# Four samples per feature product, with the products spread between table lookups, in a recommendation tower on one core

## The chip, the cores and the metric

The kernel runs on one core of one Trainium2 chip. The metric is device time in microseconds, the median of several executions. The core has TensorE (PE, matmuls), VectorE (DVE), ScalarE (ACT), GpSimd (POOL) and SyncE (SP, which only starts DMAs); each has its own in-order queue, and they meet through semaphores. Matmuls write PSUM; all other tiles are in SBUF.

## The reference

2048 samples. Each has a dense vector of 128 numbers and 26 table indices; the 26 rows looked up and the dense vector make 27 features. All 351 dot products of two different features, with the dense vector, are the 479 inputs of a three-layer perceptron.

```python
e = jnp.stack([tbl_0[ids[:, 0]], ..., tbl_25[ids[:, 25]]], axis=1)     # 2048 x 26 x 128
all_emb = jnp.concatenate([bottom_output[:, None, :], e], axis=1)      # 2048 x 27 x 128
gram = jnp.einsum('bfd,bgd->bfg', all_emb, all_emb)
z = gram[:, _TRIU_I, _TRIU_J]                                          # 351 pairs
h = jnp.concatenate([z, r_bottom_output], axis=1)
h = jnp.maximum(h @ W_top1 + b_top1, 0.0)                              # 479 -> 512
h = jnp.maximum(h @ W_top2 + b_top2, 0.0)                              # 512 -> 256
y = h @ W_top3                                                         # 256 -> 1
```

Twelve tables have 1000 rows, the others 1250 to 125000. Everything is float32.

## The kernel before

The batch is four blocks of 512 samples, each four tiles of 128. `features` holds all 27 features of a block with the 128 dimensions on the partitions: `[128, tile, sample, feature]`.

**Two ways to look up.** 18 tables are gathered: one indirect DMA on GpSimd (line 368) fetches 128 rows into `rows` (a ring of two tiles), TensorE transposes them in groups of four (`transpose_group`, line 403), and ScalarE copies each group into `features` (line 577). The other 8 tables of 1000 rows are looked up by a product (`onehot_lookups`, lines 421 and 422): the table is loaded whole (`table_raw`, 125 partitions of 4 KB, line 264) and split in a high part (ScalarE, line 596) and a low part (VectorE, line 716); the wanted indices of 512 samples are loaded on all partitions (`wanted`, line 272) and compared with the row numbers into eight one-hot chunks (seven on VectorE, line 732; one on ScalarE, lines 605 and 611); 8 chunks x 2 parts are 16 matmuls of 512 columns, and ScalarE copies the result straight into `features` (line 627). The first block looks up 12 tables in this way, four of them for 384 samples only. `table_raw` is a ring of two; a load waits until the low part of the table two before is taken.

**Products.** `gram_tile` makes one small product per sample, 26 x 26 (line 442), four samples side by side in the four 32-row quadrants of PSUM. TensorE runs all 128 of a tile in a row, and the four tiles of a block one behind the other:

```python
for i in range(P):
    at = QUADRANT * (i % 4)
    last = pe.matmul(gram[at:at + GRAM, q % 2, i // 4, 0:GRAM],
                     features[:, q, i, 0:GRAM], features[:, q, i, 1:SLOTS], start=True, stop=True)
```

ScalarE (two or three of the quadrants) and VectorE then copy columns of the products to the partitions where layer 1 wants them (`regroup`, lines 557 and 559: five copies per quadrant, one of 10 x 320 and four of 128 columns), and three small DMAs of SyncE (line 293) move the columns that don't fit. VectorE splits the result in high and low (`split_tile`), for four input tiles `pairs` plus the dense vector.

**Layers.** Layer 1 is 4 outputs x 5 inputs x 3 matmuls of 512 columns (lines 449 to 451), layer 2 is 2 x 4 x 3, the output layer two float32 products (line 509).

**Order.** It is written out by hand per block, in a hardware loop over blocks: four product tiles; then the 8 lookups of the next block; then the layers of this block; the transposes are tucked in between. PSUM holds two groups of transposes, two tiles of products and two accumulators `acc`.

## Time and profile before

| | |
|---|---|
| median of 3 runs | 464.12 us (463.21 to 467.48) |
| profiled execution, first to last instruction | 643.8 us (its own time: not given apart from this span) |
| mean granted TensorE clock in it | 0.759 |
| instructions in it | 13317 |

The profile is of one other execution, in which every instruction leaves a record. Its span is 180 us longer than the timed runs, so its stages must be weighed one by one before they are compared with 464.12 us; the section on the prediction does that.

### The profile page before, as it was taken

Reading aid. Unit: us, or ns where it says so; the run is one execution under the profiler, and the core shown is the slowest. Engines: PE = TensorE matmul, PEld = TensorE weight load, DVE = VectorE, ACT = ScalarE, POOL = GpSimd, SP = SyncE. Lnnn points to the kernel's source line nnn. Section 1 sums busy time; section 2 is a strip of 40 time slices with the busy share of each in tenths; the row PEclk is TensorE's granted clock in tenths of the full one; section 3 lists DMA queues with packets and bytes.
Section 4 is the critical chain, followed back from the end, with each engine's and each line's share of the span. In section 5 each row is a group of like instructions: output and inputs, shape, how many; then the busy total and the mean of one; then the engine's idle time right before and its main releaser. Section 6 shows DMA issues by size and latency. Waiting matters only on the chain.

```text
span 643.8 us, 13317 instructions
## 1 busy us (share of the span) xinstructions
PE 395.4 (61%) x5324; PEld 296.7 (46%) x5324; DVE 235.1 (37%) x472; ACT 310.4 (48%) x470; POOL 285.1 (44%) x282
## 2 busy tenths in 40 slices
PE   2686572353578947625367894733536799467487
PEld 2464461232466835214256673412325578335375
DVE  3574560033286411030347822002135782202451
ACT  2484660056489512223559751412456983028832
POOL 7777357556003754664600573555550067250000
PEclk9798785565699987756568998955556899677689
DMA  5558442111224411111123441111121331010000
GB/s 157 165 184 230 168 139 58 38 40 44 91 98 134 144 41 43 45 47 36 49 81 109 152 126 29 51 42 43 41 68 57 132 114 50 25 42 6 8 4 0
DMA packets 21925, 50.39 MB, mean 78 GB/s; under 512 B 7288, under 2 KB 7320, under 8 KB 21744
## 3 DMA queue, kind: packets, MB, share of 16 engines
q1 hardware_dynamic: 12902, 30.96, 14.5%
q0 software_dynamic: 8832, 18.11, 10.6%
q8 instruction: 45, 0.74, 0.5%
q10 hardware_dynamic: 138, 0.52, 0.2%
q14 instruction: 8, 0.07, 0.0%
HBM read 49.00 MB, written 0.01 MB: 76 GB/s over the span
## 4 chain that ended last, share of the span: by engine, by line
PE 37%; issue 25%; another core or an unknown queue 13%; DMA 11%; ACT 9%; DVE 3%; SPq 0%; ACTq 0%; DVEq 0%
DMA table_raw<-in_tbl 11%; PE gram L442 11%; PE acc L421 5%; PE turned L403 5%; PE acc L422 4%; PE acc L449 4%; PE acc L451 4%; PE acc L450 3%; ACT pairs L559 3%; ACT table_hi L596 2%; DVE table_lo L716 2%; ACT features L577 1%; PE acc L509 1%; DVE onehot L732 1%
## 5 line engine op out<-in xcount | busy, mean ns | idle before, releaser
L368 POOL DMA_INDIRECT rows<-in_tbl,index x276 | 284.4, 1030 | 292.3 <-PE turned L403 157.0
L442 PE MATMUL gram<-features 128*26 128x26 f32 x4096 | 94.9, 213 | 151.8 <-issue 150.1
L421 PE MATMUL acc<-onehot,table_hi 125*128 125x512 f32 (+1 forms) x288 | 127.1, 441 | 50.2 <-DVE table_lo L716 22.7
L442 PEld LDWEIGHTS gram<-features 128*26 128x26 f32 x4096 | 70.7, 128 | 185.6 <-issue 183.3
L577 ACT COPY features<-turned 128x512 f32<-128x512 f32 (+2 forms) x80 | 82.2, 1062 | 139.4 <-remote 102.7
L422 PE MATMUL acc<-onehot,table_lo 125*128 125x512 f32 (+1 forms) x288 | 121.6, 422 | 0.0
L732 DVE TENSOR_SCALAR onehot<-wanted,row_number 125x512 fp32r<-125x512 int32 (+1 forms) x252 | 104.2, 475 | 33.7 <-PE acc L422 20.1
L557 DVE COPY aside<-gram 10x320 f32<-10x320 f32 x21 | 15.5, 737 | 234.6 <-remote 177.2
L421 PEld LDWEIGHTS acc<-onehot,table_hi 125*128 125x128 f32 x288 | 60.9, 211 | 71.8 <-issue 38.4
L559 ACT COPY pairs<-gram 18x128 f32<-18x128 f32 (+3 forms) x172 | 67.2, 390 | 1.5
L422 PEld LDWEIGHTS acc<-onehot,table_lo 125*128 125x128 f32 x288 | 60.9, 211 | 10.8
L403 PE MATMUL turned<-identity,rows 128*128 128x128 f32 x276 | 56.4, 322 | 12.8 <-issue 7.6
L557 ACT COPY aside<-gram 10x320 f32<-10x320 f32 x43 | 31.3, 729 | 63.7 <-remote 42.6
L716 DVE TENSOR_TENSOR table_lo<-table_raw,table_hi 125x1024 fp32r<-125x1024 f32 x36 | 44.0, 1223 | 49.2 <-ACT table_hi L596 37.2
L596 ACT CAST table_hi<-table_raw 125x1024 fp32r<-125x1024 f32 x36 | 38.3, 1064 | 35.3 <-DMA table_raw<-in_tbl 34.9
L403 PEld LDWEIGHTS turned<-identity,rows 128*128 128x128 f32 x276 | 37.3, 162 | 21.3 <-issue 12.5
L627 ACT COPY features<-acc 128x512 f32<-128x512 f32 (+1 forms) x36 | 42.2, 1172 | 6.2 <-PE acc L422 5.3
L649 ACT ACTIVATE h<-acc,b_sb 128x512 f32<-128x512 f32 x16 | 10.7, 687 | 59.0 <-remote 37.5
L771 DVE CAST onehot<-h 128x512 fp32r<-128x512 f32 x16 | 7.0, 437 | 75.8 <-ACT h L649 50.9
L449 PE MATMUL acc<-onehot,w_hi 128*128 128x512 f32 x32 | 16.5, 516 | 26.6 <-ACT h L649 26.6
L559 DVE COPY pairs<-gram 18x128 f32<-18x128 f32 (+1 forms) x84 | 32.4, 385 | 0.9
L611 ACT ACTIVATE onehot<-distance,row_number 125x512 fp32r<-125x512 f32 (+1 forms) x36 | 25.6, 712 | 14.3 <-PE acc L422 11.8
(40 smaller groups left out, 302.1 us busy)
## 6 DMA issues: line engine op xcount, KB each, us to landing
table_raw<-in_tbl SPq DMA_DIRECT2D x35, 500.0 KB
wanted<-in_onehot_ids SPq DMA_DIRECT2D x36, 256.0 KB
rows<-in_tbl,index POOLq DMA_INDIRECT x276
aside<-in_w SPq DMA_DIRECT2D x1, 1280.0 KB
bottom<-in_xT SPq DMA_DIRECT2D x4, 256.0 KB
h<-in_w SPq DMA_DIRECT2D x1, 512.0 KB
table_raw<-in_tbl ACTq DMA_DIRECT2D x1, 500.0 KB
pairs<-aside SPq DMA_DIRECT2D x16, 20.0 KB
```

Source lines behind the costliest of these rows:

```text
L368: pool.indirect_dma_start(out=rows[:, q % RING, f, :], out_offset=None, in_=gathered[f], in_offset=bass.IndirectOffsetOnAxis(ap=index[q // ...
L403: last = pe.transpose(turned[:, n % 2, i, :], rows[:, q % RING, first + i, :], identity[:])
L421: pe.matmul(to, table_hi[0:ROW_PARTS, i % TABLE_RING, c, :], of, start=(c == 0), stop=False)
L422: last = pe.matmul(to, table_lo[0:ROW_PARTS, i % TABLE_RING, c, :], of, start=False, stop=(c == CHUNKS - 1))
L442: last = pe.matmul(gram[at:at + GRAM, q % 2, i // 4, 0:GRAM], features[:, q, i, 0:GRAM], features[:, q, i, 1:SLOTS], start=True, stop=True)
L449: pe.matmul(to, w_hi, x_hi, start=first, stop=False)
L557: copy(to(aside, 0, ASIDE, ASIDE), of(ASIDE, 1, ASIDE))
L559: last = copy(to(pairs, QUADRANT * j, COLUMN_ROWS[j], PAIR_TILES), of(COLUMN_ROWS[j], COLUMNS_FROM[j], PAIR_TILES))
L577: nc.scalar.copy(features[:, q % BLOCK_TILES, :, 1 + first:1 + first + size].rearrange("d b f -> d f b"), turned[:, n % 2, 0:size, :]).the ...
L596: nc.scalar.copy(table_hi[0:ROW_PARTS, i % TABLE_RING], table_raw[0:ROW_PARTS, i % 2]).then_inc(table_high, 1)
L716: dve.tensor_tensor(table_lo[0:ROW_PARTS, i % TABLE_RING], table_raw[0:ROW_PARTS, i % 2], table_hi[0:ROW_PARTS, i % TABLE_RING], ALU.subtr ...
L732: dve.tensor_scalar(onehot[0:ROW_PARTS, c, samples], wanted[0:ROW_PARTS, i % 2, samples], row_number[0:ROW_PARTS, c:c + 1], None, ALU.is_e ...
```

## The change

1. **Four samples per product.** `features` becomes `[128, ring of 4 tiles, pair of samples, feature, 2]`. `gram_chunk` multiplies the 4 x 27 features of four samples with their 4 x 26 features: one product of 108 x 104 in place of four of 26 x 26; only its four diagonal blocks are used. A tile is 32 products in 4 chunks of 8.
2. **Products leave through DRAM.** Each chunk is copied whole (107 partitions x 832) to `products`, two chunks of a tile by VectorE and two by ScalarE; four DMAs per tile store the diagonal blocks into a DRAM tensor `square`, and nine DMAs per part load them back as layer 1 wants them (three input tiles instead of four).
3. **Eleven lookups by product in every block** (44 in place of 36), so 15 gathered tables per tile (240 gathers in place of 276). A lookup's result is copied to a block buffer `looked`, and from there, when a block's lookups are done, one ScalarE copy per tile (`place`, 11 x 128) puts it into `features`.
4. **A table comes in two DMAs**, of 112 and 13 partitions. Its ring is three deep, and the low part is written over the raw table, so a load waits for the end of the lookup three before. The weights no longer share tiles with other data.
5. **An order for all engines.** `order()` lists the steps of the whole kernel, unrolled: the first block's 11 lookups; then the 16 chunks of a block, with a lookup of the next block, a slice of the layers of the block before (one output of layer 1, layer 2) or the output layer ahead of each chunk; a group of transposes goes in where a table of lengths says its rows have landed. The last block's chunks have only layers ahead of them, and its layers run in two halves of 256 samples; the load of the second half's pairs waits for the output of the first half, since the second layer's result lies in the same tile.

```diff
-ONEHOT = [3, 4, 9, 13, 14, 17, 20, 21]
-RING = 2
-PAIR_TILES = 4
+ONEHOT = [3, 4, 9, 13, 14, 17, 20, 21, 22, 23, 24]
+LOOKUPS = (11, 11, 11, 11)
+HIGH_RING = 2
+LOW_RING = 3
+WANTED_RING = 3
+PACK = 4
+CHUNK_GROUPS = 2 * BANK_GROUPS
+PAIR_TILES = 3
...
+LENGTH = {"lookup": 38, "gram": 16, "layer1": 27, "layer2": 52, "output": 15, "turn": 5, "place": 0}
...
+        if b == 0:
+            before = spread(lookups(1, 0, LOOKUPS[1]), len(chunks))
+        elif b < BLOCKS - 1:
+            before = (lookups(b + 1, 0, FIRST_LOOKUPS) + layers(b - 1)
+                      + behind(("output", b - 1, 0), lookups(b + 1, FIRST_LOOKUPS, LOOKUPS[b + 1])))
+        else:
+            before = [[]] * (TILE_CHUNKS + 1) + layers(b - 1) + [[("output", b - 1, 0)]]
...
-        features = sb("features", [P, BLOCK_TILES, P, SLOTS])
+        features = sb("features", [P, FEATURE_RING, P // 2, SLOTS, 2])
+        looked = sb("looked", [P, MOST, BLOCK])
...
+            of = onehot_tables[i].rearrange("(p c) d -> p c d", c=CHUNKS)
+            for at in (slice(0, EVEN_PARTS), slice(EVEN_PARTS, ROW_PARTS)):
+                eng.dma_start(table_raw[at, n % LOW_RING], of[at]).then_inc(raw_landed[n % LOW_RING], 16)
+        def store_place(eng, t, s):
+            eng.dma_start(square[b % 2, q, s],
+                          products[SLOTS * s:SLOTS * s + GRAM, t % PRODUCTS_RING, s].rearrange("f g t -> f (g t)")
...
+        def load_triple(eng, part, i):
+            eng.dma_start(pairs[row:row + n, first:end].rearrange("f q s k t -> f (q s) (k t)"),
+                          square[b % 2, first:end, :, 0:n, (g - 1) * RUN:(g - 1 + PAIR_TILES) * RUN].rearrange(
+                              "q s f n -> f (q s) n")).then_inc(pairs_landed, 16)
...
+                for i in range(CHUNK_GROUPS):
+                    at = (i % BANK_GROUPS) * WIDE
+                    a, e = divmod(j * CHUNK_GROUPS + i, 2)
+                    of = features[:, t % FEATURE_RING, a * PACK:(a + 1) * PACK, :, e]
+                    last = pe.matmul(gram[0:PACK * SLOTS, n % 2, i // BANK_GROUPS, at:at + WIDE],
+                                     of.rearrange("d s f -> d (s f)"), of[:, :, 1:SLOTS], start=True, stop=True)
...
+        def take_products(copy, t, j):
+            return copy(
+                products[0:LAST_ROW, t % PRODUCTS_RING, :, :, first:first + CHUNK_GROUPS].rearrange(
+                    "f s g (k t) -> f (s g) k t", k=2),
+                gram[0:LAST_ROW, n % 2, :, 0:BANK_GROUPS * WIDE].rearrange("f k (t n) -> f n k t", n=WIDE))
...
+            def place(t):
+                nc.scalar.copy(features[:, t % FEATURE_RING, :, SLOTS - LOOKUPS[b]:SLOTS, :].rearrange("d u f e -> d f u e"),
+                               looked[:, first:MOST, q * P:(q + 1) * P].rearrange("d f (u e) -> d f u e", e=2)
+                               ).then_inc(placed, 1)
```

What stands in a row on the engines, at three places. First TensorE. Before, the end of the loop's products in the first tile of a block, with the jump to the next pass (`ISA` and `REGISTER_ALU` rows only set up waits):

```order
L400 REGISTER_ALU
L403 MATMUL turned<-identity,rows 128x128 x4
L442 MATMUL gram<-features 26x26 x16
L398 ISA
L400 REGISTER_ALU
L403 MATMUL turned<-identity,rows 128x128 x2
L442 MATMUL gram<-features 26x26 x48
L543 REGISTER_ALU
L543 COMPARE_AND_BRANCH
```

Now, between two lookups of block 2 and with products of block 1:

```order
L457 MATMUL acc<-onehot,table_hi 128x512
L458 MATMUL acc<-onehot,table_lo 128x512
L469 MATMUL turned<-identity,rows 128x128 x4
L484 MATMUL gram<-features 108x104 x8
L469 MATMUL turned<-identity,rows 128x128 x4
L457 MATMUL acc<-onehot,table_hi 128x512
```

The products stood in long runs with nothing but transposes between them; now a chunk of eight stands behind every lookup or slice of a layer.

Second SyncE. Before, the moves of a tile's columns, inside the loop:

```order
L293 DMA pairs<-aside 10x512
L293 DMA pairs<-aside 6x512
L293 DMA pairs<-aside 2x256
L246 REGISTER_ALU
L264 DMA table_raw<-in_tbl 125x1024
```

Now, where the pairs of block 0 are loaded:

```order
L330 DMA table_raw<-in_tbl 112x1024
L330 DMA table_raw<-in_tbl 13x1024
L342 DMA pairs<-square 26x16x96
L342 DMA pairs<-square 24x16x96
L342 DMA pairs<-square 20x16x96
L342 DMA pairs<-square 18x16x96
L342 DMA pairs<-square 14x16x96
L342 DMA pairs<-square 11x16x96
L342 DMA pairs<-square 8x16x96
L342 DMA pairs<-square 5x16x96
L342 DMA pairs<-square 2x16x96
L361 DMA wanted<-in_onehot_ids 128x512
```

Nine loads stand in one piece in the queue that also brings the tables and the wanted indices.

Third ScalarE. Now, at the change from block 0's lookups to its products:

```order
L575 CAST table_hi<-table_raw 125x1024
L562 COPY features<-turned 128x4x64x2
L603 COPY features<-looked 128x11x64x2 x4
L581 ACTIVATE distance<-wanted,row_number 125x512
L586 ACTIVATE onehot<-distance,row_number 125x512
```

The four copies of `place` stand in a row, ahead of the one-hot chunk of a later lookup. Before, such copies were spread, one behind each lookup (line 627).

## Rows read from the trace of the kernel before

**Rows 1.** The page: busy us of each engine (share of span), instructions.

```profile
PE 395.4 (61%) x5324; PEld 296.7 (46%) x5324; DVE 235.1 (37%) x472; ACT 310.4 (48%) x470; POOL 285.1 (44%) x282
```

**Rows 2.** Windows by stage: length, busy time (instructions) per engine, clock, DMA share, GB/s.

```profile
0.00:90.00 90.00, 55.27 (x224) 44.12 (x227) 50.90 (x101) 51.69 (x61) 58.82 (x57) 0.89 0.56 172
90.00:175.00 85.00, 34.21 (x1057) 24.29 (x1058) 17.95 (x35) 30.75 (x56) 46.01 (x46) 0.57 0.23 66
175.00:249.50 74.50, 59.71 (x248) 46.64 (x248) 37.59 (x75) 41.19 (x56) 27.77 (x27) 0.89 0.29 91
249.50:332.30 82.80, 36.94 (x1065) 24.55 (x1064) 16.09 (x33) 33.52 (x60) 44.06 (x46) 0.58 0.20 58
...
566.50:611.00 44.50, 26.25 (x1065) 18.37 (x1064) 10.87 (x24) 28.71 (x54) 8.95 (x10) 0.73 0.08 19
611.00:643.80 32.80, 26.28 (x119) 20.51 (x112) 10.92 (x22) 8.86 (x17) 0.00 (x0) 0.89 0.01 3
```

**Rows 3.** Timeline, TensorE, product stages: start, length, engine, line, [idle before].

```profile
406.91 0.41 PE L442 MATMUL gram<-features 128*26 128x26 f32 x32
...
417.36 0.29 PE L442 MATMUL gram<-features 128*26 128x26 f32 x3 [1.18 <-issue]
...
602.86 1.74 PE L442 MATMUL gram<-features 128*26 128x26 f32 x127 [2.47 <-issue]
```

**Rows 4.** Chain that ended last, from 0 to 90 us: shares, then start, length.

```profile
by line: DMA table_raw<-in_tbl 60.4%; issue 11.7%; DVE table_lo L716 6.9%; ACT table_hi L596 5.9%; PE acc L421 4.2%; PE acc L422 3.9%; DVE onehot L732 2.7%; ACT features L627 1.0%; SPq L272 0.8%; SPq L299 0.5%; SPq L297 0.5%; PE turned L403
...
2.15 11.75 DMA table_raw<-in_tbl
...
57.45 14.80 DMA table_raw<-in_tbl
```

**Rows 5.** Chain from 185 to 200 us: start, length.

```profile
193.86 6.64 DMA table_raw<-in_tbl
```

**Rows 6.** Lines by form: busy us, mean ns of one, idle before and its releasers.

```profile
L368 POOL DMA_INDIRECT rows<-in_tbl,index x276 | 284.4, 1030 | 292.3 <-PE turned L403 157.0 <-issue 79.0 <-DMA index<-in_ids 41.4
...
L577 ACT COPY features<-turned 128x512 f32<-128x512 f32 x61 | 71.8, 1197 | 106.7 <-remote 72.4 <-PE turned L403 33.0 <-ACT y_sb L665 1.2
...
L716 DVE TENSOR_TENSOR table_lo<-table_raw,table_hi 125x1024 fp32r<-125x1024 f32 x36 | 44.0, 1223 | 49.2 <-ACT table_hi L596 37.2 <-issue 11.9
...
L596 ACT CAST table_hi<-table_raw 125x1024 fp32r<-125x1024 f32 x36 | 38.3, 1064 | 35.3 <-DMA table_raw<-in_tbl 34.9 <-issue 0.2
...
L403 PEld LDWEIGHTS turned<-identity,rows 128*128 128x128 f32 x276 | 37.3, 162 | 21.3 <-issue 12.5 <-ACT features L577 2.5
...
L557 ACT COPY aside<-gram 10x320 f32<-10x320 f32 x43 | 31.3, 729 | 63.7 <-remote 42.6 <-PE gram L442 20.8
...
L559 ACT COPY pairs<-gram 18x128 f32<-18x128 f32 x43 | 18.4, 428 | 0.0
...
L649 ACT ACTIVATE h<-acc,b_sb 128x512 f32<-128x512 f32 x16 | 10.7, 687 | 59.0 <-remote 37.5 <-PE acc L451 21.5
```

**Rows 7.** Timeline, VectorE: the seven one-hot chunks of a lookup.

```profile
338.98 2.86 DVE L732 TENSOR_SCALAR onehot<-wanted,row_number 125x512 fp32r<-125x512 int32 x7
```

**Rows 8.** Timeline, TensorE at 352 us: lookup matmuls around four transposes.

```profile
352.58 0.39 PE L422 MATMUL acc<-onehot,table_lo 125*128 125x512 f32 x1
352.81 0.60 PE L403 MATMUL turned<-identity,rows 128*128 128x128 f32 x4
353.16 0.47 PE L421 MATMUL acc<-onehot,table_hi 125*128 125x512 f32 x1
353.48 0.40 PE L422 MATMUL acc<-onehot,table_lo 125*128 125x512 f32 x1
```

**Rows 9.** Timeline, TensorE: the float32 product of the output layer.

```profile
408.77 1.45 PE L509 MATMUL acc<-aside,w_sb 128*1 128x512 f32 x3
```

**Rows 10.** Timeline at the end: SyncE's moves of columns, VectorE behind them.

```profile
615.52 2.14 SPq L293 DMA_DIRECT2D pairs<-aside  x3
...
618.82 0.43 DVE L762 CAST pairs_hi<-pairs 128x512 fp32r<-128x512 f32 x1 [2.19 <-DMA pairs<-aside]
```

More of the change, by code:

```diff
@@ L88, with groups_of, products_and_others, lookups @@
 ACT = mybir.ActivationFunctionType
-def dlrm_tower(nc, xT, ids, onehot_ids, row_numbers, gathered, onehot_tables, w1, b1, w2, b2, w3, out):
+def groups_of(t):
+    n = TABLES - LOOKUPS[t // BLOCK_TILES]
+    return [min(GROUP, n - g) for g in range(0, n, GROUP)]
+LENGTH = {"lookup": 38, "gram": 16, "layer1": 27, "layer2": 52, "output": 15, "turn": 5, "place": 0}
+FIRST_LOOKUPS = 5
+GATHER_LENGTH = 14
+GATHER_START = 60
+def products_and_others():
+    def lookups(b, first, last):
+        return [[("lookup", b, i)] for i in range(first, last)]
+    def layers(part):
+        return [[("layer1", part, m)] for m in range(M1)] + [[("layer2", part, 0)]]
+    def behind(output, others):
+        return [[output] + others[0]] + others[1:]
+    def spread(others, n):
+        places = [[] for _ in range(n)]
+        for i, other in enumerate(others):
+            places[i * n // len(others)] = other
+        return places
+    steps = [step for place in lookups(0, 0, LOOKUPS[0]) for step in place]
+    for b in range(BLOCKS):
+        first = b * BLOCK_TILES
+        steps += [("place", first + q, 0) for q in range(BLOCK_TILES)]
+        chunks = [("gram", first + q, j) for q in range(BLOCK_TILES) for j in range(TILE_CHUNKS)]
+        if b == 0:
[5 more added lines that the diff above has]
+            before = [[]] * (TILE_CHUNKS + 1) + layers(b - 1) + [[("output", b - 1, 0)]]
+        for i, chunk in enumerate(chunks):
+            steps += before[i] if i < len(before) else []
+            steps.append(chunk)
+    for part in range(BLOCKS - 1, len(PARTS)):
+        steps += [step for place in layers(part) for step in place] + [("output", part, 0)]
+    return steps
@@ new lines, with accumulations @@
+ORDER = order()
+LOOKUP_STEPS = [step for step in ORDER if step[0] == "lookup"]
+def accumulations():
+    number = {}
+    for kind, b, i in ORDER:
+        if kind in ("lookup", "layer1", "output"):
+            number[kind, b, i] = len(number)
+        if kind == "layer2":
+            for m in range(M2):
+                number[kind, b, m] = len(number)
+    return number
+FILL = accumulations()
+PAIRS_AFTER = {("gram", (b + 1) * BLOCK_TILES, 1): b for b in range(BLOCKS - 1)}
+PAIRS_AFTER["gram", TILES - 1, 0] = len(PARTS) - 2
@@ new lines, in load_pairs @@
+            def load_pairs(part):
+                b, first, end = PARTS[part]
+                for t in range(b * BLOCK_TILES + end - PRODUCTS_RING, b * BLOCK_TILES + end):
+                    sp.wait_ge(square_landed[t % PRODUCTS_RING], (t // PRODUCTS_RING + 1) * PACK * 16)
+                if part:
+                    sp.wait_ge(acc_out, FILL["output", part - 1, 0] + 1)
+                for i in range(len(TRIPLES)):
+                    load_triple(sp, part, i)
+            load_index(0)
+            load_wanted(0)
@@ new lines, in output @@
+            def output(part):
+                fill, (b, first, end) = FILL["output", part, 0], PARTS[part]
+                act.wait_ge(accumulated, fill + 1)
+                at_least(act, out_landed, 16 * part)
+                nc.scalar.copy(y_sb[:, 0:width(part)].rearrange("o (q a s e) -> o q s a e", q=end - first, s=PACK, e=2),
+                               acc[0:1, fill % 2, 0:width(part)].rearrange("o (q s a e) -> o q s a e", q=end - first, s=PACK, e=2)
+                               ).then_inc(acc_out, 1)
+                act.wait_ge(acc_out, fill + 1)
+                at = b * BLOCK + first * P
+                act.dma_start(out[:, at:at + width(part)], y_sb[:, 0:width(part)]).then_inc(out_landed, 16)
```

959 lines of the change are left out of this document (410 added, 549 removed).

## The prediction

> **What bounds the kernel now.** I read the windows by stage first, then the chain of waits, then the lines by form. Over the whole span no engine is full: TensorE 61%, ScalarE 48%, GpSimd 44% [rows 1]. The windows [rows 2] show why: stages with different limits. In the first 90 us TensorE is busy for 55. Each later block is a product stage of 83 to 85 us with TensorE busy for 34 to 37 at a granted clock of 0.57 (mostly the lower level, 1.2 GHz), and then lookups and layers, 74.5 us with 59.7 busy at 0.89. The last product stage takes 44.5, the tail 32.8.
>
> The span is 643.8 us and the median 464.12, so 180 us of the profile are not in the timed runs. All other stages together are 90 + 3 x 74.6 + 32.8 = 347 us (the third window of lookups repeats the first), the product stages 297. In these, 32 product records run in 0.41 us, 10.6 ns apart up to the next group, and elsewhere three records end a wait of 1.18 us for nothing that the profile shows [rows 3]. This is the only stage with enough such waiting to lose 180 us, so I put the loss there: the timed runs have 464 - 347 = 117 us for four product stages and for whatever lies outside the span, 27 to 29 us a block. ScalarE's work in such a stage is 31 to 33.5 us, and 28.7 in the last [rows 2]: it sums to 126, as much as is left for them. So in the timed runs the copies behind the products fill the product stage, while TensorE needs 1024 records x 10.6 ns = 11 us of it per block. What lies outside the span is then small; I take 8 us, between 0 and 15.
>
> The first 90 us hang on the tables: 60.4% of the chain there is the load of tables, one of them 14.80 us, where a table alone later takes 6.64 [rows 4, 5].
>
> **The change part by part**, made against the 347 + 117 us above.
>
> *Step lengths at the upper clock.* Lookup matmuls start 0.233 us apart [rows 8] (352.58 to 352.81), so a lookup is 16 x 0.233 = 3.73 us. Four transposes put 353.48 - 352.81 - 0.233 = 0.44 us between them, 0.11 each, 1.65 for a tile of 15. A layer matmul has the same 512 columns: layer 1 is 48 x 0.233 = 11.2, layer 2 24 x 0.233 = 5.6. Float32 records of 512 columns take (1.45 - 0.16) / 3 = 0.43 us, with 0.16 for the pipeline's end [rows 9], so the output layer's four are 1.7.
>
> *The product.* The trace has no 108 x 104 product. At 0.84 ns per column [rows 9] a record of 104 columns is 87 ns, two per product. Whether the 108-column weight load hides is the question: around a float32 transpose of 128 columns it does, nearly (107 ns at that rate, 110 measured [rows 8]). I take 90 ns: a chunk is 16 x 0.09 = 1.44 us, a block 23.0, the kernel 1024 x 0.09 = 92 us. Bounds: 87 ns, and 162 ns more, the mean of a transpose's weight load [rows 6], if it is never hidden. I take the transposes' spacing, the nearest row. Before, the quadrants overlapped and TensorE needed 44 us; so its own work grows by 48 us here.
>
> The Trainium skill speaks against this part. "TensorEngine Tiling (Array Packing)", sections Available Configurations and Performance Considerations: an array cut into four column tiles of 32 works on them independently, up to four times as fast for a small output dimension. By that rule the change gives the factor of four up. The 10.6 ns of [rows 3] for what would be 22 ns in a row at 0.84 ns a column agree in direction. The same page says that copying PSUM out may then become the bound, and the 126 us of ScalarE agree with that too.
>
> *Copies out of the products.* Before, a tile was four copies of 320 (0.729 us) and sixteen of 128 (0.428) [rows 6]: up to 9.8 us. The two sizes give 1.57 ns per element and 0.23 fixed; 832 elements are 1.54 us, and 1.8 at the feature copy's rate (1.197 us for 512); I take 1.65, four per tile 6.6, shared by two engines. Bounds: 1.0 us, by the unstrided ReLU of 512 in 0.687 [rows 6], and 1.9 us. ScalarE's share falls from some 100 us to 32 x 1.65 = 53. They now have 5 to 6 us of other TensorE work between them, so at either bound they are hidden.
>
> *Eight more lookups, 36 fewer gathers.* A lookup costs TensorE 3.73 us. Gathers cost GpSimd (284.4 + 79.0) / 276 = 1.32 us [rows 6]; 240 are 316 us, continuous, always ahead of the 400 us and more that TensorE takes. Its 157.0 us of waiting for transposes says that it has room.
>
> *First stage.* Three tables are in flight and a ring place is free at a lookup's end: period = (load + high 1.06 + low 1.22 + lookup 3.73) / 3. With loads of 8 us (between 6.64 and 14.80 [rows 4, 5]) it is 4.67 us. VectorE needs 1.22 + 2.86 = 4.1 [rows 6, 7]. So 11 x 4.67 = 51; the first table lands at 2.15 + 6.64 = 9 (the second one before at 13.9 [rows 4]), its parts take 2.3: the stage ends at 63 us, against 90. Bounds: 4.1 and 6 us a lookup, 57 to 78.
> The Trainium skill, "DMA: Bandwidth & Descriptors", section "Why a DMA increments its semaphore by 16 and not by 1": a DMA uses the largest number of engines up to 16 that divides its outermost dimension. 125 partitions would get 5 engines, 112 get 16. By that rule the load is no longer late and the stage goes by VectorE, ending 6 us earlier; the DMA share of 0.56 [rows 2] with late tables doesn't contradict it.
>
> *Blocks.* Block 0's products: 41.0 (lookups) + 23.0 + 6.6 (transposes) = 70.6. Blocks 1 and 2 add 11.2 + 5.6 + 1.7: 89.1 each. The last: 23.0 + 6.6 + 18.5 = 48.1. On top come waits in the sequence: (a) the split of the pairs ahead of layer 1 takes 3 x 1.1 us on VectorE (0.43 [rows 10] and half of a 1.22 us low part [rows 6]) behind a product copy, and TensorE has 0.7 us of bottom work meanwhile: 3 us in each of blocks 1 and 2; (b) four copies of `place` stand in a row on ScalarE; 1408 elements are 1.55 us each unstrided, 2.8 at the 1.197 us per 512 of the feature copy [rows 6]. Behind them waits the one-hot chunk of the lookup after next. From the last lookup's end ScalarE has 0.9 + 1.65 + 6.2 (or 11.2) + 1.4 = 10.2 (15.2) us to it; TensorE's chunk, lookup, chunk and transposes, and 5 of 8 parts of the next lookup, are 9.5: 1 to 6 us. In the last block no lookup covers the first copy: 4 us; (c) handovers. Before, lookups and layers of 8 x 3.73 + 60 x 0.233 + 5.6 + 4 of transposes = 53.5 took 74.5, 21 of waiting; the chunks now fill the ones behind ReLU and split, so I take 3 to 5. Together: 77, 96, 96, 52. VectorE in such a block has 11 x 4.1 + 8 x 1.65 + 9 of splits = 67 us; ScalarE 11 x 3.2 (high 1.06, and abs, one-hot and copy like the ReLU, 0.7 each) + 11 of feature copies + 6 of `place` + 13 of products + 4 of ReLU = 69 us: both below 89.
>
> *SyncE.* Each move of columns costs 2.14 / 3 = 0.71 us of issue [rows 10]; nine loads are 6.4 us, and tables and wanted indices queue behind them. These run three lookups ahead, 17 us, so I cost it at nothing; without that cover it would be 6 us in blocks 1 and 2. Stores wait for their chunks and only delay loads that are early.
>
> *Tail.* Before 32.8. Now two halves in series: 72 matmuls of 256 columns at 0.12 are 8.6, handovers 4, output 0.9: 13.5 each. Between them the loads of the second half's pairs wait for the first half's output: 6.4 + 2.19 + split 1 = 9.6. Sum 37.
>
> Total: 63 + 77 + 96 + 96 + 52 + 37 = 421, and 8 outside: 429, **forecast 430 us**, a gain of 34: 27 from the first stage, and 8 from the rest, 224 + 109 + 33 = 366 before and 77 + 96 + 96 + 52 + 37 = 358 now.
>
> **Rivals.**
> 1. *No waits.* (a) to (c) vanish and tables come by VectorE's pace: 57 + 71 + 90 + 90 + 49 + 34 + 8 = 399 to 412. For it: chunks between all steps. Against: 21 us in 74.5 before. Chance 0.22.
> 2. *ScalarE becomes the bound.* If the pair-wise feature copies stay at 1.8 ns per element, ScalarE has 35 + 17 + 11 + 14 + 4 = 81 us in a block, block 0 goes by it (82), and each block change costs 6: 445 to 457. The block buffer then doesn't do what it should. For it: 1.197 us per 512 in [rows 6], a stride as well. Chance 0.16.
> 3. *Slower than before: weight loads show in the products.* Each product record waits for its load. 34 us over 1024 records are 33 ns: at 123 ns per record it is as slow as before, with half of the 162 ns exposed (171 ns) 430 + 83 = 513. For it: no run of 108-column loads behind such short products is in this trace. Against: the transposes. Chance 0.14, with other losses of that size in the row of steps.
> 4. *The profile's loss is elsewhere.* Then the product stages really take more than 29 us and the gain is larger; this ends in rival 1's range.
>
> **How the numbers follow.** Forecast 430 (418 to 443): 0.48. Rival 1: 0.22, of it 0.05 below 396. Rival 2: 0.16. Rival 3: 0.14, of it a part below 466. The range that leaves out 2 in 10 is 396 to 466. About 1% is what a measurement of this kernel can tell; that is 459.5 and 468.8. Faster by over 1%: 0.48 + 0.22 + 0.16 = 0.86, of which 0.07 goes to no change, since rival 2 ends at that limit; with 0.01 of rival 3 that is 0.79, 0.08 and 0.13 for slower.
>
> **What would show it.** The chunk of eight products 1.4 to 1.5 us long in the timeline; the first chunk at 63 us; copies to `products` about 1.65 us, `place` 1.55; TensorE busy over 85% of the time between 63 us and the last chunk, at a clock near 1; no wait of TensorE for rows; profile and timed runs closer together, since the records fall by more than half. It is wrong if chunks take over 1.9 us, if TensorE waits for ScalarE at each block change by more than 6 us, or if the tail exceeds 45.

## The result and the profile after

The changed kernel takes 438.27 us (median of 4 runs, 431.13 to 439.86), the kernel before 464.59 (4 runs, 463.21 to 467.48): ratio 0.935, 95% interval 0.926 to 0.944. (Executions fall in a faster and a slower state; ratios, here and below, are of the runs in the faster one, medians are of all runs.) Forecast: 430. The profiled execution is the fastest of the four: 431.13 us, of which the span is 429.1.

The page of after: busy time, TensorE in 40 slices, its granted clock, the chain that ended last.

```profile
PE 384.5 (90%) x2348; PEld 325.2 (76%) x2348; DVE 256.1 (60%) x480; ACT 234.2 (55%) x326; POOL 287.6 (67%) x246
...
PE   0999999997699986899999999899999789997847
...
PEclk9999999999699999999999999999999998999979
...
PE 49%; POOL 28%; issue 7%; DMA 6%; DVE 3%; ACT 3%; SPq 3%; DVEq 0%; ACTq 0%; POOLq 0%
```

TensorE went from 61% to 90% [rows 1] and its clock from 0.759 to 0.98. New in the chain is GpSimd with 28%: the gathers.

Windows of after, cut where the first product of each block starts and the last ends (length, busy time of PE, PEld, DVE, ACT, POOL, clock, DMA share, GB/s), beside [rows 2]:

```profile
0.00:63.00 63.00, 51.76 (x222) 41.09 (x223) 52.04 (x105) 42.78 (x58) 48.43 (x42) 1.00 0.83 216
63.00:146.70 83.70, 75.50 (x488) 66.01 (x487) 59.24 (x108) 55.81 (x75) 68.77 (x50) 0.96 0.67 180
146.70:247.70 101.00, 94.23 (x577) 78.99 (x576) 62.65 (x116) 57.02 (x82) 79.06 (x73) 1.00 0.62 155
247.70:341.80 94.10, 90.10 (x559) 75.71 (x557) 55.15 (x101) 53.18 (x78) 74.28 (x66) 1.00 0.55 137
341.80:393.50 51.70, 49.55 (x360) 43.16 (x361) 17.36 (x24) 18.35 (x24) 17.10 (x19) 0.97 0.30 70
393.50:429.10 35.60, 23.34 (x152) 20.22 (x151) 9.71 (x28) 7.12 (x15) 0.00 (x0) 0.90 0.10 25
```

The same stretches were forecast at 63, 77, 96, 96, 52 and 37 us.

Lines by form of after (busy us, mean ns of one, idle before and its releasers), beside [rows 6]:

```profile
L440 POOL DMA_INDIRECT rows<-in_tbl,index x240 | 287.0, 1196 | 76.0 <-issue 71.9 <-DMA index<-in_ids 3.1 <-PE turned L469 0.9
...
L550 DVE COPY products<-gram 107x832 f32<-107x832 f32 x32 | 32.8, 1024 | 51.3 <-PE gram L484 51.2
L562 ACT COPY features<-turned 128x512 f32<-128x512 f32 x48 | 30.9, 644 | 6.3 <-PE turned L469 6.2
L550 ACT COPY products<-gram 107x832 f32<-107x832 f32 x32 | 27.4, 855 | 19.7 <-PE gram L484 19.6
...
L603 ACT COPY features<-looked 128x1408 f32<-128x1408 f32 x16 | 23.2, 1545 | 0.0
```

The gathers, now 240 in place of 276, wait for TensorE for 0.9 us in place of 157.0: GpSimd runs without a stop from 4.6 us to its last gather at 363.4, one gather per 1.50 us. What TensorE waited for in after (us in total, times, longest):

```profile
PE acc L489 <- DVE pairs_lo L717: 13.1, 10, 5.4
PE turned L469 <- DMA rows<-in_tbl,index: 12.6, 5, 6.5
PE acc L457 <- DVE table_lo L675: 10.4, 1, 10.4
PE gram L484 <- issue: 2.4, 1, 2.4
```

Timeline at the end of after: 48 products in a row, the two output layers, and between them SyncE's second load of pairs.

```profile
383.61 9.86 PE L484 MATMUL gram<-features 128*108 128x104 f32 x96
...
406.80 1.02 PE L528 MATMUL acc<-pairs,w_sb 128*1 128x256 f32 x4 [0.57 <-ACT pairs L617]
...
413.82 0.58 PE L489 MATMUL acc<-pairs_hi,w_hi 128*128 128x256 f32 x1 [5.45 <-DVE pairs_lo L717]
...
426.11 1.02 PE L528 MATMUL acc<-pairs,w_sb 128*1 128x256 f32 x4 [0.57 <-ACT pairs L617]
...
408.35 3.33 SPq L342 DMA_DIRECT2D pairs<-square  x9
```

### The profile page after: what moved, and what is told of

Same layout as the page of the kernel before. It is cut to its first block, busy times and chain, and to the rows that moved or that the text cites. A ratio compares the mean times of both kernels' runs of the same rounds, so it can differ in the third digit from the quotient of the medians.

```text
span 429.1 us, 6585 instructions
## 1 busy us (share of the span) xinstructions
PE 384.5 (90%) x2348; PEld 325.2 (76%) x2348; DVE 256.1 (60%) x480; ACT 234.2 (55%) x326; POOL 287.6 (67%) x246
## 4 chain that ended last, share of the span: by engine, by line
PE 49%; POOL 28%; issue 7%; DMA 6%; DVE 3%; ACT 3%; SPq 3%; DVEq 0%; ACTq 0%; POOLq 0%
POOL rows L440 28%; PE gram L484 13%; PE acc L457 8%; PE acc L458 8%; PE acc L489 5%; PE acc L490 5%; PE acc L491 5%; PE turned L469 4%; SPq L342 2%; DMA rows<-in_tbl,index 2%; DMA pairs<-square 2%; DVE pairs_lo L717 2%; PE acc L528 2%; ACT features L603 1%; DVE pairs_hi L715 1%
## 5 line engine op out<-in xcount | busy, mean ns | idle before, releaser
L457 PE MATMUL acc<-onehot,table_hi 125*128 125x512 f32 x352 | 145.0, 412 | 12.3 <-DVE table_lo L675 10.4
L688 DVE TENSOR_SCALAR onehot<-wanted,row_number 125x512 fp32r<-125x512 int32 x308 | 131.2, 488 | 30.2 <-PE acc L458 14.8
L458 PE MATMUL acc<-onehot,table_lo 125*128 125x512 f32 x352 | 140.9, 400 | 0.0
L484 PE MATMUL gram<-features 128*108 128x104 f32 x1024 | 112.4, 263 | 2.4 <-issue 2.4
L484 PEld LDWEIGHTS gram<-features 128*108 128x108 f32 x1024 | 109.2, 180 | 4.5 <-issue 3.4
L550 DVE COPY products<-gram 107x832 f32<-107x832 f32 x32 | 32.8, 1024 | 51.3 <-PE gram L484 51.2
L586 ACT ACTIVATE onehot<-distance,row_number 125x512 fp32r<-125x512 f32 x44 | 31.9, 725 | 45.4 <-PE acc L458 44.7
L469 PE MATMUL turned<-identity,rows 128*128 128x128 f32 x240 | 37.7, 277 | 12.6 <-DMA rows<-in_tbl,index 12.6
L562 ACT COPY features<-turned 128x512 f32<-128x512 f32 x64 | 39.3, 614 | 15.2 <-PE turned L469 15.1
L550 ACT COPY products<-gram 107x832 f32<-107x832 f32 x32 | 27.4, 855 | 19.7 <-PE gram L484 19.6
L581 ACT ACTIVATE distance<-wanted,row_number 125x512 f32<-125x512 int32 x44 | 32.0, 727 | 0.8 <-ACT y_sb L625 0.8
L594 ACT COPY looked<-acc 128x512 f32<-128x512 f32 x44 | 25.6, 583 | 11.1 <-PE acc L458 7.2
```

What stands on the lines that cost most here:

```text
L457: pe.matmul(to, table_hi[0:ROW_PARTS, n % HIGH_RING, c, :], of, start=(c == 0), stop=False)
L458: last = pe.matmul(to, table_lo[0:ROW_PARTS, n % LOW_RING, c, :], of, start=False, stop=(c == CHUNKS - 1))
L469: last = pe.transpose(turned[:, n % 2, i, :], rows[:, t % ROWS_RING, GROUP * g + i, :], identity[:])
L484: last = pe.matmul(gram[0:PACK * SLOTS, n % 2, i // BANK_GROUPS, at:at + WIDE], of.rearrange("d s f -> d (s f)"), of[:, :, 1:SLOTS], start ...
L550: return copy(products[0:LAST_ROW, t % PRODUCTS_RING, :, :, first:first + CHUNK_GROUPS].rearrange("f s g (k t) -> f (s g) k t", k=2), gram ...
L562: nc.scalar.copy(features[:, t % FEATURE_RING, :, 1 + GROUP * g:1 + GROUP * g + size, :].rearrange("d u f e -> d f u e"), turned[:, n % 2, ...
```

## Experiments

All twelve ran where the kernel before took 648.4 to 652.4 us (four groups of 7 to 11 runs, on three chips) and the changed kernel 479.76, not 464.59 and 438.27. What is different there, the runs don't tell. So each time below is read beside those, by its ratio to the kernel before in the same group.

### The changed kernel there (c_after)

> The changed kernel itself, beside the kernel before on the same chip as the three that follow. The runs of the first four experiments had the kernel before at 650 us in place of 464, with TensorE waiting up to 29 us for nothing that the profile shows, so they need a comparison on their own chip. If this chip is like the one of the result: 438 us, ratio 0.935. If it is like that of the first four experiments: before 650, this 470 to 480, ratio 0.73.

479.76 us (472.66 to 484.13); before 648.4; ratio 0.732 (0.726 to 0.737). Most of the 41 us more than in the result lies in one kind of stretch (the longest at 103 to 127 us, another at 180 to 193). Timeline of this run, TensorE, GpSimd and ScalarE:

```profile
104.68 0.40 PE L458 MATMUL acc<-onehot,table_lo 125*128 125x512 f32 x1
...
111.75 0.33 PE L484 MATMUL gram<-features 128*108 128x104 f32 x1 [0.90 <-issue]
111.90 0.94 POOL L440 DMA_INDIRECT rows<-in_tbl,index  x1 [0.30 <-issue]
113.16 0.48 PE L484 MATMUL gram<-features 128*108 128x104 f32 x1 [1.08 <-issue]
...
127.14 1.05 PE L484 MATMUL gram<-features 128*108 128x104 f32 x5 [0.37 <-issue]
127.44 0.72 ACT L586 ACTIVATE onehot<-distance,row_number 125x512 fp32r<-125x512 f32 x1 [20.99 <-remote]
...
127.76 1.77 POOL L440 DMA_INDIRECT rows<-in_tbl,index  x1 [4.93 <-remote]
```

From 103 to 127 us TensorE starts few records, from 106 us on one at a time, at distances that are multiples of 0.70 us, and waits for nothing that the profile shows. The gathers beside it run at their shortest, 0.94 us with 0.30 between. GpSimd stops at 122.8, and TensorE is free again from 127.

TensorE is not the only one that is held. ScalarE's one-hot chunk of 127.44 needed only its own `distance` (through at 106.4) and the end of TensorE's lookup, whose last matmul started at 104.68; it still started 21 us late. VectorE stands for 29.54 us up to 126.46, and GpSimd's wait of 4.93 us can only be for transposes, which were through by 110.0. The gathers' rhythm alone isn't enough either. The window just before has the same rhythm, with TensorE busy for 4.84 of 5 us:

```profile
98.00:103.00 5.00, 4.84 (x33) 3.96 (x31) 0.00 (x0) 0.50 (x1) 3.78 (x4) 1.00 0.77 212
```

The wait named "issue" is 29.4 us of the products here and 2.4 in the result's profile. The name also covers waits with a plain cause: the 2.37 us in the result's profile (at 341.75) end as ScalarE is through with the first copy of `place` (four of them from 340.22), and so do 4.08 us (at 173.65) and 2.37 us (at 388.08) of the 29.4. The trace of the kernel before had stretches of the same kind, and I had not looked at both engines together:

```profile
111.93 0.94 POOL L368 DMA_INDIRECT rows<-in_tbl,index  x1 [0.30 <-issue]
117.70 0.94 POOL L368 DMA_INDIRECT rows<-in_tbl,index  x1 [4.83 <-PE turned L403]
...
113.88 0.20 PE L442 MATMUL gram<-features 128*26 128x26 f32 x1 [1.20 <-issue]
...
116.82 1.22 PE L442 MATMUL gram<-features 128*26 128x26 f32 x82
```

82 records run in 1.22 us in the pause of GpSimd from 112.9 to 117.7, about 3 us into it; while it gathers, from 96 to 113 us, they come in ones to fives.

### Without gathers, both kernels (e11, e12)

```diff
-            for t in range(TILES):          # e11, GpSimd
+            for t in range(ROWS_RING):
-                pe.wait_ge(rows_landed[t % ROWS_RING][g], rows_count(t, g))
+                pe.wait_ge(rows_landed[t % ROWS_RING][g], rows_count(t % ROWS_RING, g))
...
-            with pool.Fori(1, BLOCKS) as b:   # e12: only tiles 0 and 1 of block 0 are gathered
```

> The changed kernel with the gathers of the first two tiles alone (30 of 240); the later tiles use the same rows again, so the 210 other gathers are left out, and all else of the computation stays. On a chip where the kernel before takes 648 us and the changed one 480. Theory (GpSimd has two effects: its gathers set the pace, and while they run back to back TensorE gets one instruction per 0.70 us): both go, TensorE's waits for nothing fall from 29 us to below 5 and those for rows to 0, the time is 405 to 425 us. Rival A (GpSimd sets the pace, but the waits for nothing have another cause): 435 to 460, with 20 us and more of these waits left. Rival B (neither): 470 to 480.

> The kernel before with the gathers of the first two tiles alone (36 of 276); the later tiles use the same rows again, so 240 gathers are left out. Theory (the 150 us of waits for nothing in the products arise only beside back-to-back gathers): they go, and the time falls from 648 us to 430 to 470, what the timed runs of the result had; the product stages are then 27 to 33 us, filled by ScalarE's copies, as the prediction had them for the timed runs. Rival (4096 short products starve TensorE's instruction supply by their number, whatever GpSimd does): 600 us or more. In between: part of the waits has another cause.

e11: 416.45 us (413.23 to 425.56), ratio 0.636 (0.630 to 0.642). e12: 451.69 us (448.14 to 463.56), ratio 0.689 (0.683 to 0.696). Both times are in the range of their theory. The gathers cost the kernel before 200 us and the changed one 63 in this place. TensorE's waits in e11:

```profile
PE acc L489 <- DVE pairs_lo L717: 11.2, 5, 5.5
PE gram L484 <- issue: 2.4, 1, 2.4
```

No wait for rows, and of the waits named "issue" 0.4 us and the 2.4 that belong to `place`, as in the result's profile. In e12 the windows of the four product stages are:

```profile
87.00:119.30 32.30, 19.53 (x1056) 16.07 (x1056) 18.81 (x35) 28.19 (x52) 0.00 (x0) 0.74 0.19 58
184.90:218.00 33.10, 19.73 (x997) 15.36 (x996) 15.88 (x33) 29.87 (x55) 0.00 (x0) 0.75 0.10 32
284.00:319.00 35.00, 20.73 (x1030) 16.30 (x1030) 15.85 (x33) 31.09 (x57) 0.00 (x0) 0.73 0.12 35
382.30:415.80 33.50, 20.53 (x1066) 15.74 (x1065) 10.85 (x24) 28.63 (x54) 0.00 (x0) 0.80 0.03 6
```

32 to 35 us where [rows 2] had 83 and, for the last, 44.5, with ScalarE busy for 28 to 31: undisturbed, the copies fill the product stage. TensorE's waits named "issue" in the products fell from 150.1 to 46.9 us, not to nothing as the theory had it; ScalarE is busy during most of what is left. With the gathers of two tiles alone the change is worth 451.7 - 416.5 = 35 us.

### Fewer and more gathers (e4, e5)

```diff
-ONEHOT = [3, 4, 9, 13, 14, 17, 20, 21, 22, 23, 24]
-LOOKUPS = (11, 11, 11, 11)
+ONEHOT = [3, 4, 9, 13, 14, 17, 20, 21, 22, 23, 24, 25]    # e5: without 24
+LOOKUPS = (12, 12, 12, 12)                                # e5: 10 each
```

> The changed kernel with 12 lookups by product in each block in place of 11, so 14 gathered tables per tile, 224 gathers in place of 240; each block's twelfth lookup stands ahead of the last chunk with the step that was there. Theory (GpSimd's gathers, one per 1.5 us and continuous to 363 us, set the pace now, and TensorE's waits for rows are 12.6 us): 16 gathers fewer free 24 us on GpSimd, while TensorE has 4 lookups more (15 us) and 16 transposes fewer (1.8); the waits for rows go, and the time stays within 1% or falls by up to 5 us. Rival (TensorE is the bound, as predicted, GpSimd has room): slower by 13 us, 0.7 of them in the first stage per 1% of the lookup, so 451 us where the changed kernel takes 438, 3% more.

> The changed kernel with 10 lookups by product in each block, 16 gathered tables per tile, 256 gathers. Theory (GpSimd sets the pace): 16 gathers more are 24 us on GpSimd, the last rows land 24 us later, while the first stage ends 4.7 us earlier: 450 to 460 us where the changed kernel takes 438. Rival (TensorE is the bound): 15 - 1.8 = 13 us faster, 425 us. If both bind by turns: within 1%.

Twelve: 482.41 us, ratio 0.739 (0.735 to 0.744), against 0.732: 13 us more of TensorE work cost 2.7 us by the medians, 1% by the ratios. Ten: 505.33, ratio 0.781 (0.776 to 0.786): 25.6 us slower with 16 gathers more and 13 us of TensorE work less, 1.6 us per gather. Both times are near what the theory said and far from its rival, and eleven is near the balance there. That GpSimd's gathers set the pace by themselves the traces don't show: TensorE's waits for rows are 5.7 us in c_after, 5.1 with twelve and 10.9 with ten, while with ten GpSimd stands 44.4 us for transposes (4.4 in c_after) and TensorE 22 us for ScalarE's copies into `features` (11.6 of them once, for a `place`).

### The two DMAs of a table (e1, e2)

```diff
-            for at in (slice(0, EVEN_PARTS), slice(EVEN_PARTS, ROW_PARTS)):
-                eng.dma_start(table_raw[at, n % LOW_RING], of[at]).then_inc(raw_landed[n % LOW_RING], 16)
+            at = slice(0, ROW_PARTS)
+            eng.dma_start(table_raw[at, n % LOW_RING], of[at]).then_inc(raw_landed[n % LOW_RING], 16)
```

e2 makes the reverse edit in the kernel before.

> The changed kernel with each table in one DMA of 125 partitions in place of two of 112 and 13; nothing else differs. Theory (the two DMAs made the first stage short): a table again takes 11.75 to 14.80 us to land, as in the profile of before; with three tables in flight a lookup of the first stage then takes (11.75 to 14.8 + 1.06 + 1.22 + 3.73) / 3 = 5.9 to 6.9 us in place of 4.7, so the first chunk of products starts at 77 to 88 us in place of 63, and the time is 452 to 463 us. Rival (the third place of the ring and the low part written in place did it, the split of the DMA nothing): within 1% of the changed kernel, 434 to 442 us, the first chunk at 63 us.

> The kernel before, with each table in two DMAs of 112 and 13 partitions, as the change has it; its ring of two tables stays. If the load was what the first 90 us waited for and the split mends it, the first stage goes by VectorE's 4.1 us a lookup and ends near 63 us in place of 90: about 437 us, as fast as the changed kernel, and then all the rest of the change together is worth nothing. If a ring of two keeps the stage at half of the gain: about 450. If the split does nothing: 464.

e1 by its trace: the first products start late, as the theory had it (77 to 88):

```profile
L484 PE MATMUL gram<-features x1024: 256/262/506, 87.5 to 440.9; 128*108 128x104 f32 x171
```

With two DMAs it is 62.4 (e9) and 63 (after), so without the split nearly all of the first stage's gain is gone; ScalarE's waits for tables rise from 16.0 us (after) to 78.6 over the kernel. Yet the time is 477.42 us, ratio 0.734 (0.729 to 0.738), no change. The 25 us are won back in block 0. Its products start at 87.5 us and those of block 1 at 165.0, in c_after at 61.8 and 173.65: e1 has no stretch like the one at 103 to 127, and from 95 to 160 us TensorE is busy for 63.0 of 65 us at a clock of 1.00. So this run shows what the split does to the stage, and not what it is worth in a run like the result's. e2: 640.68 us, ratio 0.985 (0.979 to 0.991), its first products at 84.1 us in place of 90.0. That is less than half of the gain that I had given a ring of two: with two tables in the ring, and TensorE waiting 6.29 us once for nothing that the profile shows and 3.12 for a one-hot chunk, only 6 us of the stage went. The split alone is not enough.

### The order and the packing undone (e3, e10)

```diff
-        for i, chunk in enumerate(chunks):
-            steps += before[i] if i < len(before) else []
-            steps.append(chunk)
+        steps += chunks
+        for place in before:
+            steps += place
```

```diff
+                    for s in range(PACK):
+                        to = gram[QUADRANT * s:QUADRANT * s + GRAM, n % 2, i // BANK_GROUPS, at + s * GRAM:at + (s + 1) * GRAM]
+                        last = pe.matmul(to, of[:, s, 0:GRAM], of[:, s, 1:SLOTS], start=True, stop=True)
```

> The changed kernel with the 16 chunks of a block in one row, ahead of its lookups and layers, so that only the spreading of the products is undone (the dense vectors of blocks 2 and 3 are loaded behind layer 2, where their tile is free). Theory (the spreading is worth what the chunks cover): before, lookups and layers of one block had 21 us of waiting in 74.5 us for ReLU, split and table parts; I expect 5 to 8 us of it back in each of three blocks, so 453 to 462 us. Rival (with copies of 0.86 and 1.02 us per chunk of 1.60 us nothing has to be spread): 434 to 442 us, TensorE without a wait for copies within the row.

> The changed kernel with the products of one sample at a time again, 26 x 26 in the four 32-row quadrants, 4096 records in place of 1024; all the rest (chunks between steps, copies, DRAM, order) stays, and only the packing is undone. (The first two chunks also write the whole of their PSUM banks once, 16 records.) Theory A, as the prediction had it from the 10.6 ns between records: the quadrants overlap, TensorE needs 44 us in place of 102, and the time falls by as much as GpSimd's pace allows, to 400 to 425 us where the changed kernel takes 438. Theory B (many short instructions are what cost the kernel before its product stages of 83 us; TensorE is not supplied with them): slower, 480 us or more, with TensorE's waits for nothing that the profile shows inside the products.

e3: 556.73 us (547.3 to 565.9), 77 more than the changed kernel, far beyond both values. The rival fell: within the rows of products TensorE waits 20.8 us for ScalarE's copies and 7.3 for VectorE's. e10: 579.77, ratio 0.893 (0.887 to 0.900), 100 more; TensorE waits 106.4 us in its products without a releaser, in 176 places. Its timeline shows what the records can do and what they do beside gathers:

```profile
114.70 0.20 PE L490 MATMUL gram<-features 128*26 128x26 f32 x1 [0.41 <-issue]
...
124.57 0.74 PE L490 MATMUL gram<-features 128*26 128x26 f32 x64
```

64 records in 0.74 us are at most 11.6 ns each, near the 10.6 of [rows 3]: for TensorE alone the quadrants are the quicker form, 256 records or 3.0 us a tile against 6.4. Theory B held: in this place it is their number that costs. Both experiments are mixed with that loss, so they bound neither the interleaving nor the packing for a run like the result's; that stays open. In e3 GpSimd waits 79.4 us for transposes, against 4.4 in c_after: the row of products holds the transposes up, and so the gathers. In e10 it waits 138.6 us. The table that places the transposes is also made for the spread order.

### The form of the operands (e7)

```diff
+                    w = identity[:, 0:PACK * SLOTS] if t % 4 in (1, 3) else of.rearrange("d s f -> d (s f)")
+                    x = identity[:, 0:WIDE] if t % 4 in (2, 3) else of[:, :, 1:SLOTS]
```

> The changed kernel with other operands in the products, for their record time alone (its products are not the reference's): in the first tile of a block as it is; in the second the 108 weight columns are contiguous columns of the identity in place of the strided features; in the third the 104 moving columns are; in the fourth both. Measured with the changed form: 16 records in 1.60 us, 100 ns each, where 104 columns at 0.84 ns are 87. Theory A (the strided read of the moving side costs the 13 ns): 100, 100, 87, 87. Theory B (the strided weights do): 100, 87, 100, 87. Theory C (a product is bounded by a load of 108 columns and a fixed part, whatever the strides): 100 in all four.

A chunk of 16 records in each form, from its timeline (the printed length has 0.16 us for the pipeline's end):

```profile
63.70 1.76 PE L486 MATMUL gram<-features 128*108 128x104 f32 x16
...
83.75 1.71 PE L486 MATMUL gram<-features,identity 128*108 128x104 f32 x16
...
120.27 1.76 PE L486 MATMUL gram<-identity,features 128*108 128x104 f32 x16
...
262.73 1.68 PE L486 MATMUL gram<-identity 128*108 128x104 f32 x16
```

In the row names the identity stands second where it takes the place of the weights. So 100, 97, 100 and 95 ns a record: contiguous operands give back 5 of the 13 ns above 87 at most. Theory C is nearest.

### The load of the last pairs (e9), and a version that beats both (e13)

```diff
-                    sp.wait_ge(acc_out, FILL["output", part - 1, 0] + 1)
+                    sp.wait_ge(acc_out, FILL["output", min(part - 1, BLOCKS - 2), 0] + 1)
...
-                for g, size in enumerate(groups_of(t)):        # e13 only, GpSimd; AHEAD = 3
-                    if t >= ROWS_RING:
...
+                    at_least(pool, transposed, groups_before(t) + g - AHEAD)
```

The landing of the last pairs gets its own semaphore. What stands ahead of the prediction on this wait (the second layer's result lies in the same tile) is true of the tensor, not of its parts: the halves use different quarters of it. It served the count of one semaphore.

> The changed kernel, where the load of the last half's pairs waits for the output of block 2 in place of that of the first half of block 3 (the landing has a semaphore of its own). In the profile of after TensorE waits 5.45 us for these pairs between the two halves (413.82 us), and the loads are issued only at 408.35 us, though the products they move are stored at 395.93. Theory: they then land near 404 us, VectorE splits them before TensorE is through with the first half, and the time falls by 5 to 5.5 us, to 433. Rival: the loads collide with the stores or VectorE's split comes between the splits of the first half and delays them, and less than 2 us is gained (436 to 438).

> The changed kernel with two edits: the earlier load of the last pairs (which took the part from the last chunks to the end from 46.4 to 38.2 us in the profiles), and GpSimd held to TensorE's pace: a group of gathers starts only when TensorE has transposed all groups but the last three, where the rings allowed five to seven. Theory (back-to-back gathers that run ahead keep TensorE from its instructions, and each such stretch lasts until GpSimd's ring is full, 24 us at 103 to 127 us): stretches get shorter, TensorE's waits for nothing fall from 29 us to 10 or 15, and the time is 450 to 460 us beside 648 to 652 of the kernel before, 0.70 of it. Rival (GpSimd sets the pace and every stop of it is lost): the held gathers cost what the shorter stretches give, 470 to 475 us, the gain of the last pairs alone, or more.

e9: 476.13 us (465.85 to 489.67), ratio 0.722 (0.715 to 0.728), beside 0.732 (0.726 to 0.737): the intervals touch. The trace is clearer, since the end has no gathers. From the last row of products to the end it takes 475.6 - 437.37 = 38.2 us against 46.35 in c_after and 45.5 in after, and between the output layers:

```profile
461.46 1.02 PE L528 MATMUL acc<-pairs,w_sb 128*1 128x256 f32 x4 [0.57 <-ACT pairs L617]
472.64 1.02 PE L528 MATMUL acc<-pairs,w_sb 128*1 128x256 f32 x4 [0.57 <-ACT pairs L617]
...
451.19 3.33 SPq L342 DMA_DIRECT2D pairs<-square  x9
```

11.2 us in place of 19.3 (19.5 in c_after): 8 us, more than the 5.45 of the one wait. The rest fits TensorE's clock. First the second half in after, then in e9 (windows):

```profile
413.80:426.20 12.40, 11.25 (x70) 10.83 (x71) 4.10 (x12) 2.74 (x6) 0.00 (x0) 0.78 0.01 1
```

```profile
461.50:472.60 11.10, 10.01 (x76) 8.89 (x76) 4.33 (x13) 3.14 (x7) 0.00 (x0) 1.00 0.01 2
```

Behind the wait of 5.45 us the granted clock is 0.78 over the next 12.4 us (0.77 in c_after, where e9 ran), so part of them ran at the lower level, 1.2 GHz; without the wait it is 1.00.

e13: 467.1 us (463.8 to 471.16), ratio 0.714 (0.710 to 0.717), 2.4% below the changed kernel, with intervals apart. Its waits:

```profile
POOL rows L436 <- PE turned L465: 34.5, 11, 6.7
PE gram L480 <- issue: 21.0, 7, 12.6
```

TensorE's waits named "issue" in the products went from 29.4 to 21.0 us, not to 10 or 15 as the theory had it, and GpSimd now stands for 34.5 us. Of the 21.0 us 19.1 are two waits that end with the first copy of a `place`, at 163.68 and 382.49. The longer one comes behind a stretch of the known kind, beside gathers in a row up to 158.4, in which ScalarE too was held:

```profile
161.35 0.85 ACT L546 COPY products<-gram 107x832 f32<-107x832 f32 x1 [13.50 <-remote]
162.10 5.64 ACT L599 COPY features<-looked 128x1408 f32<-128x1408 f32 x4
...
163.68 3.18 PE L480 MATMUL gram<-features 128*108 128x104 f32 x16 [12.62 <-issue]
```

(The chunk of products that ScalarE copies at 161.35 was through by 145.5.) So the stretch got shorter, 12 to 14 us in place of 24, and is still there. The time lies between the two values. How much of it is the held gathers and how much the last pairs, these two runs don't separate: 467 stands beside 476, and the intervals of e13 and e9 overlap. It was not run where the result was, so how it does there stays open.

## Why the prediction was right, and where not

- **Stages.** 63, 77, 96, 96, 52, 37 and 8 outside, against 63.0, 83.7, 101.0, 94.1, 51.7, 35.6 and 2.0. Sum 429 against 431.1 in the profiled execution; the median of the runs is 7 us above that, at clocks of 0.96 to 0.97 in place of 0.98. That the sum came so near is in part luck, since its errors cancel: the products took 11 us more, the waits for rows 12.6 more, against that the waits of the next point took 16 less and what lies outside the span 6 less.
- **Waits (a) to (c), too high.** For the stages of the products I had added 24 us of them (6.4, 6.9, 6.9 and 3.9). TensorE's waits there, rows left out, are 8.4: 1.5 us ahead of layer 1 in each of blocks 1 and 2 where I took 3, 2.1 in the last, 2.37 for the first copy of `place` in the last block where I took 4, no other wait for it where I took 1 to 6, and 0.9 for a one-hot chunk. In this rival 1 was nearer than I; what it left out are the rows and the longer records.
- **Tail, right, with two errors.** The nine loads are issued in 3.33 us (at 408.35) where I took 6.4 from the 0.71 of [rows 10]; against that the second half ran at a clock of 0.78, which took about 2.7 us (e9).
- **First stage, shown.** I took 4.67 us a lookup; from the first lookup at 10.4 us to the first product at 63.0 it is 4.8. That it hung on the tables is shown by e1: with one DMA of 125 partitions 87.5 us, with two 63. What the stage gives to the whole time was not shown apart. By the rule of the Trainium skill, "DMA: Bandwidth & Descriptors", section "Why a DMA increments its semaphore by 16 and not by 1", 125 partitions would get 5 engines; e1's 78.6 us of waiting for tables against 16.0 agree with it.
- **The product, mis-sized.** I took 90 ns from the transposes' spacing; 96 records in 9.86 - 0.16 us are 101 ns, so 103 us in place of 92, 11 more. At most 5 ns of it are the strides (e7).
- **Array tiling.** The rule of the Trainium skill, "TensorEngine Tiling (Array Packing)", section "Theoretical Speedup", is that tiling by four is up to four times as fast for a small dimension. It agrees in direction with e10, 3.0 us a tile against 6.4, a factor of 2.1. It was still right to weigh it low: before, the copies filled the stage (e12).
- **Copies, right in effect.** I took 1.65 us; they are 1.02 (VectorE) and 0.855 (ScalarE), at and below the lower bound of 1.0. `place` is 1.545, as forecast (1.55; the two terms of the unstrided copy give 0.23 + 1408 x 0.89 ns = 1.49). The feature copies fell to 0.644 under the new layout, which rival 2 needed to stay at 1.2.
- **Gathers, wrong.** "240 are 316 us, continuous, always ahead" was the step that failed. They take 1.50 us each, 359 us, and TensorE waits 12.6 us for rows where I said it wouldn't. A gather is 0.94 to 1.10 us where VectorE is idle (61 of them) and on average 1.196 here, where it is busy 60% of the time, with 0.30 us to the next; I had taken 1.32 with that pause, from a kernel with VectorE at 37%. One wait for rows of 6.5 us (at 110.64) and 256 records 10 ns longer (2.6 us) are more than block 0's 6.7 us; in block 1 three more waits for rows (5.3 us) and the records stand beside its 5.
- **The 180 us of the profile, right place, no cause.** I put them into the product stages and left them out. e12 shows both: those stages are 32 to 35 us when nothing disturbs them, and most of the 180 us arise only beside the gathers, a loss that the timed runs of the result did not have and those of the experiments did (648 to 652 us). My 27 to 29 us a stage were too low: the 126 us of ScalarE's work that I set against them don't fit into 117, and less into 109. Outside the span lie 2 us, not 8; the stages were longer by as much.
- **Rivals.** Rival 3 fell: a record is 101 ns, so the load is hidden but for 14 ns at most. Rival 4 was nearer to an important thing than its one sentence: where the loss does exist in timed runs, the change gains 27%, not 6%.

## What to carry to other kernels

When one profiled execution is far longer than the timed runs, look at the other engines' rows in the very stretches where the bound engine waits for nothing: a stretch that goes away when that engine's work is left out is a collision, and it may be in the timed runs elsewhere. A wait without a named cause is not always one: see first what the other engines finish at the moment when it ends. A kernel with fewer, larger TensorE instructions is safer there than one with many small ones, even if the small ones are quicker (e10). Before engines are balanced, give each its duration under the load that the changed kernel makes. And where such stretches exist, a time without change doesn't show that an edit does nothing: e1 lost 25 us in its first stage and won them back where a stretch stayed away.

## What the runs showed of the hardware

- Beside gathers of 0.94 us at intervals of 1.25, TensorE started records at multiples of 0.70 us; 3 to 4 us after the gathers stopped it ran freely, 82 short records in 1.22 us. ScalarE was held too, 21 us behind the lookup that it waited for (c_after, 127.44). It was not so from 98 to 103 us of the same run, nor in the result's profile, where gathers run in the same rhythm from 108 to 121 us. Which resource is shared was not shown.
- In such a stretch the granted clock was 0.50 (110 to 130 us in c_after), the lower level, while TensorE was mostly idle; over the result's profile it was 0.98. Behind the one wait of 5.45 us in the tail it was 0.78.
- A gather's time on GpSimd went from 0.94 to 5.36 us (at 131.42 in c_after, beside three subtractions of VectorE in a row, 2.28, 1.22 and 1.22 us). With VectorE idle 91 gathers of that run took 0.94 to 1.10 us.
- A float32 record of 104 columns with a load of 108 took 95 to 101 ns (e7 and after), where long records give 0.84 ns a column, 87 ns.
